# Second attention of a Perceiver block: the softmax denominators move from VectorE's running sum into TensorE's weighing

## The reference

```python
hidden = jnp.concatenate([context, latents], axis=1)
q = (latents @ Wq.T); k = (hidden @ Wk.T); v = (hidden @ Wv.T)      # 16 heads; 4 key/value heads of 96
scores = jnp.einsum('bkgqd,bksd->bkgqs', q, k) * scale
attn = jax.nn.softmax(scores.astype(jnp.float32), axis=-1).astype(q.dtype)
out = jnp.einsum('bkgqs,bksd->bkgqd', attn, v)
return out.reshape(...) @ Wo.T
```

## Time and profile before

| what | us |
| --- | --- |
| median of three executions | 4295.67 (4290.4 to 4313.48) |
| the profiled execution | 4310.48 |
| its span | 4308.7 |
| PE busy in the span | 3636.9 (84%) |
| VectorE busy | 2328.9 (54%) |
| GpSimd busy | 1396.8 (32%) |
| ScalarE busy | 1356.4 (31%) |
| fifteen batches of the second attention, from the first exponential's sum of the first batch (1719.44) to that of the last (3398.01) | 1678.57 |

### The profile page before, as it was taken

One profiled execution on the slowest core, in us unless ns is written; L12 is line 12 of the kernel. 1 busy time (PEld: TensorE's weight loads), 2 busy tenths in 40 slices (PEclk: granted clock), 3 DMA queues, 4 the chain that ended last, 5 costly groups with the idle time before them and its releaser, 6 DMA issues. The chain is left out here.

```text
span 4308.7 us, 72516 instructions
## 1 busy us (share of the span) xinstructions
PE 3636.9 (84%) x31360; PEld 2407.9 (56%) x31360; DVE 2328.9 (54%) x2671; ACT 1356.4 (31%) x1764; POOL 1396.8 (32%) x892
## 2 busy tenths in 40 slices
PE   6999999996566469999999999999999989575678
PEld 3566666663222345777777777777777744322224
DVE  3666556553399652444444444444444325598972
ACT  1555555554243011222222222222222102344430
POOL 4344444440098110111111111111111002496970
PEclk8999999997689789999999999999999999687999
DMA  6455455442221032111111111111111210221211
GB/s 187 123 143 137 136 142 139 135 125 37 52 81 62 20 129 79 37 35 37 37 35 40 32 44 37 37 44 37 44 37 40 79 64 3 67 81 56 79 51 37
DMA packets 216517, 303.62 MB, mean 70 GB/s; under 512 B 64856, under 2 KB 161688, under 8 KB 214792
## 3 DMA queue, kind: packets, MB, share of 16 engines
q1 hardware_dynamic: 216200, 299.00, 23.8%
HBM read 245.38 MB, written 53.10 MB: 69 GB/s over the span
## 5 line engine op out<-in xcount | busy, mean ns | idle before, releaser
L1336 POOL TENSOR_TENSOR D_ctx_lo<-D_ctx_raw,D_ctx_hi 128x1904 fp32r<-128x1904 f32 x64 | 255.6, 3994 | 1386.5 <-ACT D_ctx_hi L1330 1386.5
L580 DVE TENSOR_REDUCE A_mxc<-A_psX 128x2 f32<-128x768 f32 (+2 forms) x512 | 489.4, 990 | 267.2 <-PE A_psX L610 264.9
L800 ACT ACTIVATE A_probs<-A_psE 128x1024 f32<-128x1024 f32 (+1 forms) x416 | 426.5, 1025 | 329.4 <-PE A_psE L824 323.4
L1354 ACT ACTIVATE D_V<-D_psY 119x384 f32<-119x384 f32 x224 | 110.1, 491 | 957.8 <-PE D_psY L1421 957.8
L1370 DVE TENSOR_REDUCE D_mxc<-D_psE 128x4 f32<-128x1904 f32 (+1 forms) x128 | 242.4, 1894 | 259.1 <-PE D_psE L1440 258.9
L234 POOL TENSOR_TENSOR ES_dBx<-E_du,E_Bn 128x512 f32<-128x512 f32 x256 | 317.6, 1281 | 70.9 <-POOLq L49 69.0
L1652 ACT ACTIVATE D_probs<-D_psE 119x2048 f32<-119x2048 f32 x112 | 210.6, 1880 | 406.2 <-PE D_psE L1773 406.2
L1787 PE MATMUL D_psO<-D_probs,D_V 119*32 119x256 f32 (+1 forms) x5376 | 331.0, 397 | 0.0
L1697 DVE TENSOR_TENSOR D_acc<-D_acc,D_probs 119x1024 f32<-119x1024 f32 x96 | 117.7, 1226 | 379.9 <-ACT D_probs L1652 379.9
L1421 PE MATMUL D_psY<-D_wv_hi,D_ctx_hi 128*119 128x384 f32 (+1 forms) x896 | 313.5, 350 | 7.5 <-ACT D_V L1354 6.6
L1421 PE MATMUL D_psY<-D_wv_hi,D_ctx_lo 128*119 128x384 f32 (+1 forms) x896 | 302.2, 337 | 0.0
(11 more groups left out here) (310 smaller groups left out, 7393.3 us busy)
## 6 DMA issues: line engine op xcount, KB each, us to landing
D_ctx_raw<-in_ctx SPq DMA_DIRECT2D x48, 952.0 KB, 5.2
A_land<-in_ctx SPq DMA_DIRECT2D x32, 768.0 KB, 5.3
A_land<-in_ctx SPq DMA_DIRECT2D x16, 1024.0 KB, 5.5
E_Bn<-bc_scratch SPq DMA_DIRECT2D x64, 256.0 KB, 3.6
E_Cn<-bc_scratch SPq DMA_DIRECT2D x64, 256.0 KB, 3.4
k_scratch<-A_Khl SPq DMA_DIRECT2D x32, 384.0 KB, 5.5
A_Kst<-k_scratch SPq DMA_DIRECT2D x64, 192.0 KB, 3.6
A_land<-in_ctx SPq DMA_DIRECT2D x16, 642.0 KB, 4.3
```

Of the source, the lines that this page charges most:

```text
L580: nc.vector.tensor_reduce(mxc[:, u % 4, :, u // 4], psX[:, x % 2, :, 0:w], axis=AX_X, op=ALU.max).then_inc(x_free, 1)
L800: nc.scalar.activation(probs[0:KW[k], n % NPR, :, :].rearrange("p h q -> p (h q)"), psE[0:KW[k], :], ACT.Exp, scale=HD ** -0.5).then_inc(e ...
L1336: nc.gpsimd.tensor_tensor(ctx_lo[c][:, :, 0:w], ctx_raw[c][:, :, 0:w], ctx_hi[c][:, :, 0:w].bitcast(F32), ALU.subtract).then_inc(lo_done[c ...
```

## The change

VectorE's `add_up` goes, with its tile `acc` and its semaphore `summed`. `denominators` goes, with `den_done`. Instead `weigh` runs over four slots in place of three: for slot 3 the stationary block is `ones` where the other slots have V, so that the sum over the keys of the same 119x256 probabilities is accumulated in `psO[:, 3, :]`, in 2 x 4 more products a step. `normalise` waits for the batch's last weighing. ACT's exponential waits for the weighing alone.

```diff
@@ exponentials (ACT)
                     if N >= NPR:
                         act.wait_ge(w_done, N - NPR + 1)
-                        act.wait_ge(summed, N - NPR + 1)
@@ VectorE
-                def add_up(j, n):
-
-                    N = NU * j + n
-                    tile = [probs[:, N % NPR, :, bass.ts(i, NQ)] for i in range(2)]
-                    dve.wait_ge(e_free, N + 1)
-                    rows = [KWD[2 * n + i] for i in range(2)]
-                    if n == 0:
...
-                    dve.wait_ge(summed, N)
-                    link(nc.vector.tensor_tensor(acc[0:KR, :, :], acc[0:KR, :, :], tile[0][0:KR], ALU.add))
-                    nc.vector.tensor_tensor(acc[0:rows[1], :, :], acc[0:rows[1], :, :], tile[1][0:rows[1]], ALU.add
-                                            ).then_inc(summed, 1)
-
                 def normalise(j):
-                    dve.wait_ge(den_done, j + 1)
+                    dve.wait_ge(w_done, NU * (j + 1))
...
-                    add_up(j, 0)
-                    for n in range(1, 4):
-                        add_up(j, n)
-                        keys_out(dve, link, nxt, 0, n - 1)
+                    for t in range(T):
+                        keys_out(dve, link, nxt, 0, t)
                     read_maxima(dve, nxt, 0)
                     read_maxima(dve, nxt, 1)
-                    for n in range(4, 7):
-                        add_up(j, n)
-                        keys_out(dve, link, nxt, 1, n - 4)
+                    for t in range(T):
+                        keys_out(dve, link, nxt, 1, t)
@@ weigh and denominators (PE)
-                        for t in range(T):
+                        for t in range(T + 1):
                             for h in range(H):
                                 last = nc.tensor.matmul(psO[32 * h:32 * h + 32, t, :],
-                                                        V[0:KWD[k], k, h, bass.ts(t, 32)],
+                                                        V[0:KWD[k], k, h, bass.ts(t, 32)] if t < T
+                                                        else ones[0:KWD[k], :],
                                                         probs[0:KWD[k], N % NPR, h, bass.ts(i, NQ)],
...
-                def denominators(j):
-                    pe.wait_ge(summed, NU * (j + 1))
-                    for h in range(H):
-                        last = nc.tensor.matmul(psO[32 * h:32 * h + 32, T, :], ones[0:KR, :], acc[0:KR, h, :],
...
                     maxima(pe, nxt, 3)
-                    denominators(j)
                     for t in range(T):
                         keys(pe, nxt, 2, t)
```

More of the change, by code:

```diff
@@ L1297, in l1_attention @@
         e_full, e_free, x_full, x_free = r.sem("e_full"), r.sem("e_free"), r.sem("x_full"), r.sem("x_free")
-        mp_ready, w_done, summed, den_done = r.sem("mp_ready"), r.sem("w_done"), r.sem("summed"), r.sem("den_done")
+        mp_ready, w_done = r.sem("mp_ready"), r.sem("w_done")
         normed = r.sem("normed")
@@ L1576, in l1_attention @@
         OT = r.sb("OT", [P, M, 2, S])
-        acc = r.sb("acc", [P, H, NQ])
         psE = r.ps("psE", [P, H, 512])
@@ L1682, in _ @@
                 link.n = 2 + NKEY + 2
-                def add_up(j, n):
-                    N = NU * j + n
-                    tile = [probs[:, N % NPR, :, bass.ts(i, NQ)] for i in range(2)]
-                    dve.wait_ge(e_free, N + 1)
-                    rows = [KWD[2 * n + i] for i in range(2)]
-                    if n == 0:
-                        if j:
-                            dve.wait_ge(den_done, j)
-                        nc.vector.tensor_tensor(acc[0:KR, :, :], tile[0][0:KR], tile[1][0:KR], ALU.add
-                                                ).then_inc(summed, 1)
-                        return
-                    dve.wait_ge(summed, N)
-                    link(nc.vector.tensor_tensor(acc[0:KR, :, :], acc[0:KR, :, :], tile[0][0:KR], ALU.add))
-                    nc.vector.tensor_tensor(acc[0:rows[1], :, :], acc[0:rows[1], :, :], tile[1][0:rows[1]], ALU.add
-                                            ).then_inc(summed, 1)
                 def normalise(j):
-                    dve.wait_ge(den_done, j + 1)
+                    dve.wait_ge(w_done, NU * (j + 1))
                     link(nc.vector.reciprocal(recip[:, :], psO[:, T, :]))
@@ L1738, in _ @@
                     rows_out(dve, nxt)
-                for n in range(4):
-                    add_up(B - 1, n)
                 dve.wait_ge(x_in, 16)
[L1742 to L1745, removed]
+                for u in range(4):
+                    residual(u)
                 normalise(B - 1)
@@ L1792, in weigh @@
                     last.then_inc(w_done, 1)
-                def denominators(j):
-                    pe.wait_ge(summed, NU * (j + 1))
-                    for h in range(H):
-                        last = nc.tensor.matmul(psO[32 * h:32 * h + 32, T, :], ones[0:KR, :], acc[0:KR, h, :],
-                                                start=False, stop=True, skip_group_check=True,
-                                                tile_position=(0, 32 * h))
-                    last.then_inc(den_done, 1)
                 def project(u):
```

## The result

The changed kernel is slower, as forecast. Its first four executions took 4351.77, 4351.78, 4352.53 and 4355.09 us, median 4352.15; with one more the kernel before has a median of 4299.62 (4290.4 to 4313.48). The ratio is 1.0123, interval 1.0098 to 1.0149: +52.5 us on the medians, where +63.6 was forecast. Five further executions of the same kernel gave a median of 4364.5 and a ratio of 1.0148 (1.0121 to 1.0174), +68 us on the medians of that comparison (4296.22 before).

A forecast was written before the change was run, and what follows sets the result against it. TensorE (PE) was taken to bound the fifteen repeating batches. 96.6 - 0.4 - 13.9 - 18.7 = +63.6 us, added to a base of 4299, gave 4363 us (forecast's chance 0.69), range 4344 to 4387.

The forecast's parts named there:

- The bound: Fifteen repeating batches: TensorE bounds them, PE busy 1585.46 of 1678.57 us; VectorE can take time only in PE's few gaps.
- The price of the groups, +96.6: Weighings on PE: 224 added groups of four products at 0.431 us each, all on the path, +96.6 us.
- the quotient of a whole weighing: Bound on a group's price from the whole weighing, 2.73 / 6 = 0.455 us, which would give 101.9 us.
- the lone product: Bound on a group's price from the old product with ones standing alone, 0.57 us, which would give 127.7 us.
- The removed denominators: One PE group fewer a batch: 0.4 us back in the last batch, nothing in fifteen, where third keys wait anyway.
- Rival 2: Behind maxima 3: the removed denominators' time comes back, 15 x 0.57 = 8.6 us less, 4354 us; chance 0.09.
- The first gap: PE's gap ahead of maxima 0 shrinks from 2.45 to 1.52 us without VectorE's additions, -13.9 us over fifteen batches.
- the clock: Weighing behind the first gap: with that gap at 1.52, all fifteen batches run at clock 1.00, -18.7 us.
- slow batches that remain: Stated sign of a wrong forecast, in the changed kernel's profile: any batches remaining at clock 0.98.
- Rival 1: Behind the gap ahead of maxima 0: the clock still falls, 18.7 us more, 4381 us; chance 0.14.
- The waits that change: Exponential waits for the weighing three steps back, `normalise` for weighing 6; both done in time, so 0 us.
- The range: Whole execution: from 4344 us (rival 2 on the fastest base) to 4387 us (rival 1 and some base spread).

The follow-up runs named there:

- doubling: Changed kernel with the group of ones issued twice for each key tile, against the kernel before: ratio 1.037, fastest execution 4450.29 us.
- the second profile of the changed kernel: Changed kernel run again unedited, five further executions against the kernel before: median 4364.5 us, ratio 1.0148; one batch took 117.06 us, thirteen 115.8.

## Why the prediction was right

- *The bound.* Right. Work came to the engine that bounds the stage and left one that waits. The page's sums didn't show it; the batches did.
- *The price of the groups, +96.6.* Right, and confirmed apart: 0.431 by doubling, 3.59 us a weighing. The two readings that agreed in the trace of before were worth more than the quotient of a whole weighing (0.455) or the lone product (0.57).
- *The removed denominators, 0 in fifteen batches.* Right, and the cause shown: the third keys wait 0.58 longer at the end of the chain (0.77 in place of 0.19), and with the division out of the chain the time comes back, 0.58 of the 1.04 us a batch. Rival 2 fell.
- *The first gap, -13.9, and the clock, -18.7.* Both amounts came out: gaps of 1.52, every batch of the first profile at 1.00. The cause given was wrong, so that the amount of the gap was right by luck. The prediction credited the gap to the removal from VectorE. It then saw that the keys end 0.86 later, but used this only to clear GpSimd's subtraction, and never asked whether the longer weighing alone would hide the held addition. It does: with the additions kept, the gap is 1.59 and the time the same. Each of the two edits suffices by itself (the removal alone: 1.52 too), and together they give it once. The sum was right since it counted the gap once.
- *The clock as a term.* Shown by holding the gap: the falls return. That a gap of 1.52 lets it fall never was too strong; one batch of fourteen was longer by 1.2 to 1.3 us in five of the nine profiles in which no gap was over 1.61 us, each time with a fall of the clock right behind a gap of 1.53. The prediction named slow batches that remain as a sign of being wrong, and the second profile of the changed kernel has one, the 117.06 above. Rival 1 is therefore right in kind and small in size.
- *The waits that change, 0.* Right: no new wait of PE's appears.
- *The range.* The fifteen batches came out at +59.3 us and the last batch at +5.6, against 57.9 and 5.6. The first comparison gave 52.5 and the second 68; between the first two profiles 19.5 us lie in the first attention, which the change does not touch. The decision to keep that spread out of the sum and put it on the base held, but that the two comparisons lie on either side of 63.6 is chance. The lower end of the range is 4345 by its own terms (4290.4 + 55), not 4344; nothing hangs on it.

What stays open is why the first attention is granted a low clock more often in some executions than in others, and what besides the gap decides how often the clock falls. That GpSimd's subtraction is what holds the addition rests on the two standing together each time; no run took the subtraction away.

## What to carry to other kernels

Read a cost where it is paid: the same group of four products, 0.43 us, costs 0.43 in a full stream and some 0.1 in a gap, and nothing comes back where it is removed ahead of a chain that is late anyway. Before giving work to the bounding engine to free another, look for the one instruction of the other that is late, and move that; here moving one pair of additions won 33 us, and moving all the work lost some 64. And when two edits of one change could each close a gap, count it once and test them apart before naming the cause.

## What the runs showed of the hardware

- A group of four fp32 products on four column groups (119x32 by 119x256) costs 0.431 us behind its like, even with operands that the group ahead just used. Four groups between other shapes take 1.86, 0.14 more than 4 x 0.431, the same 0.14 as between 0.57 and 0.43 in the earlier trace rows; no run shows what the 0.14 is made of.
- TensorE's granted clock fell to 1.2 GHz behind a gap of 2.45 us in eleven and twelve of fourteen batches (110.7 us without a fall), behind a gap of 2.41 in six of fourteen batches (116.7 us without one), and at times behind one of 1.52 or 1.53. A fall cost 1.6 to 1.7 us behind the long gap and 1.2 to 1.3 behind the short one.
- A VectorE addition with both inputs in SBUF that was issued 0.06 us after a GpSimd subtraction of 2.24 us took 3.26 us instead of 1.23, in each of the fifteen batches of the kernel before. In the same profile an addition that had begun 0.74 us ahead of a GpSimd subtraction (1727.66 against 1728.40) took its usual 1.23. The cast and the subtraction that read PSUM inside a GpSimd subtraction of 4.65 us were not held.
